# One kernel, four small edits: the column sum of the values on GpSimd and in slot 6, the gelu table asked for early, the second inverse roots moved, and fill products in the first image

## The chip, the cores and the metric

The kernel runs on one core of one Trainium2 chip. The metric is the device time of one execution, in microseconds. The median of three runs before the change is 2034.94 us (2033.91 to 2036.55). The profiled execution took 2021.73 us, with a span of 2020.0 us from the first to the last instruction.

The engines are called by the profile's names: PE (TensorE, the matmuls), PEld (its weight loads), DVE (VectorE), ACT (ScalarE), POOL (GpSimd), SP (SyncE, which here only issues DMAs).

## What is computed

Sixteen images and sixteen texts of 128 tokens go through a small model. Cut to what matters:

```
h  = concat(edge_filter(image) [256 rows x 256], (U*s @ Vt)[text ids] [128 rows x 256])   # 384 rows
h  = h + attention(layernorm(h))       # 16 heads of 16, window of 128 keys back
h  = h + gated_block(layernorm(h))     # gelu(x @ w_block) in the 288 best rows, x in the others
h  = h + state_space(layernorm(h))     # circulant recurrence over the rows
h  = h + shared_ffn(x) + two_of_eight_experts(x),  x = layernorm(h)

attn = softmax(scores) + 1e-9          # so ctx = softmax @ v + 1e-9 * (sum of v over all 384 rows)
ffn(x) = gelu(x @ w1.T + b1) @ w2.T + b2
layernorm(x) = (x - mean) / sqrt(var + 1e-5)
```

The 1e-9 matters for this change: every row of the attention's output gets 1e-9 times the sum of all value rows, and the kernel computes that sum.

## The kernel before, in words

**Two halves.** The first (to about 1400 us of the span) goes through the images, one after another; the second does the experts in chunks of 256 rows. The change touches the first half only.

**Slots.** One image's attention is cut into 24 units (3 tiles of 128 query rows, 8 pairs of heads). `sequence(b, ...)`, which exists once for each engine, walks through 33 slots (`SLOTS`, s from 0 to 32), and in each it writes out, in a fixed order, what the engine does there: in slot s the scores of unit s on PE, its row maximum on DVE, its exp on ACT, then the transposes of the probabilities of unit s-2 on PE and their copy out of PSUM on ACT. Every fourth slot, 6, 10, 14 and so on, has the products of four units' probabilities with the values. Slots 0 to 7 work on 128 keys, slots 8 to 23 on 256 keys. Between these lie, in fixed slots, the pieces of three other images: the tail ("chain") of image b-1, that is gate, block, state space and router; the second half of the shared feed-forward of image b-2 (`DOWNS`: six pieces in slots 2, 3, 4, 5, 7 and 8); and the head of image b+1, that is edges, text rows, projections. Engines meet through semaphores only. Each engine works strictly in its own written order, so an instruction that waits holds up everything behind it.

The trip of the steady images, b = 2 to 13 or 14, is a loop. Images 0 and 1 and the last ones are written out apart. Image 0 has no chain and no shared feed-forward around it; there DVE also works out, in slots 1 to 10, the powers of the rotation for the state space (`eigenvalues`, `powers`), many small steps each waiting for the last.

**What the change touches.**

- `values_sum`: PE multiplies a constant matrix (`ones9`, all 1e-9) with the three tiles of values in `vaug`, adding up in PSUM bank 5. Tile 0 is done in slot 1 (`TURN0`), tiles 1 and 2 in slot 2 (`BLOCK`). DVE copies the result to `sumv` in slot 2. It is first read in slot 13.
- Slots 1 and 2 of PE: turned rows of the chain (`turn_chain`), the scores 1, the ranks of image b-2 (`slot_ranks`), then the row of gate scores (line 1840), the block's product (line 1790), and the first piece of the shared feed-forward (line 1813). That last piece waits until ACT has read the block's product through gelu (`g`, line 876), since both lie in the same banks.
- ACT holds one table of functions at a time. Exp and gelu are in different ones. In every image the exp's table is loaded behind `g`, and the gelu's ahead of the first `hidden_layer` (line 885, slot 30), behind the copy `cxT` (line 857). On PE `up(b, f)` (line 1800) makes the hidden layer's product f in one of two banks in turn; `up(b, 2)` waits until ACT has read product 0.
- `deviations` on DVE: eleven small steps on 3 numbers a row (lines 1087 to 1093), each waiting for the one before. For the chain's second layernorm they stand behind the row maximum of slot 8, while the statistics (lines 1075 to 1079) stand in slot 7 ahead of the maximum of slot 7. Their result is used in slot 11 (`chain_scale`), whose rows PE turns in slot 12 (line 1785).
- `keep_warm(n)`: PE multiplies the identity with itself n times into a bank that nobody reads.
- POOL's `sequence`: the six scattered stores of `dispatch`, then the direct term and one part of the states, inverse roots for the head, the residuals, and last in the image the gather of text rows and `hbo` (line 641).

## Time and profile before

| what | us |
|---|---|
| median of three runs | 2034.94 |
| lowest, highest | 2033.91, 2036.55 |
| profiled execution: its time | 2021.73 |
| profiled execution: span | 2020.0 |
| PE busy | 1887.5 (93% of the span) |
| DVE busy | 1395.3 (69%) |
| ACT busy | 1068.6 (53%) |
| POOL busy | 741.4 (37%) |
| one steady image (from the text product at 704.28 to the next at 785.00) | 80.72 |

A row of a timeline has the start, the time, the engine, the line and operation with output and input, how many in a row, and in square brackets how long the engine had been idle before it and who ended that. PE's own instructions overlap: the next may start before the modelled end of the last, so the distance from start to start is what one takes of the engine. A row of stretches has from and to, the length, the busy time of PE, PEld, DVE, ACT and POOL with their counts, PE's granted clock (1.00 is 2.4 GHz, 0.50 is 1.2 GHz), the DMA's share and GB/s.

### The profile page before, as it was taken

What the parts mean: (1) busy time and instruction counts of PE and PEld (TensorE: products, weight loads), DVE (VectorE), ACT (ScalarE), POOL (GpSimd) and SP (SyncE); (2) the same over time, 40 slices, a digit from 0 to 9 for tenths busy, and PEclk for the clock granted to TensorE, in tenths of its full rate; (3) what the DMA queues carried; (4) which work ended last, traced back from release to release, by engine and by line L of the source; (5) the groups of instructions that cost most, each with busy time, mean ns of one, the idle gap of its engine ahead of it and who ended that gap; (6) DMA issues with size and microseconds to landing.
All of it is one profiled execution on the core that took longest, in us unless ns stands there. A gap on an engine that the chain in (4) does not pass through costs nothing.

```text
span 2020.0 us, 46113 instructions
## 1 busy us (share of the span) xinstructions
PE 1887.5 (93%) x14343; PEld 1639.6 (81%) x14344; DVE 1395.3 (69%) x3963; ACT 1068.6 (53%) x2511; POOL 741.4 (37%) x1074
## 2 busy tenths in 40 slices
PE   5769999999999999999999999888999999999997
PEld 5557787777777877777778777677999999999997
DVE  6768778777787787787877876764765565655653
ACT  1545556556555565565555655622655555645643
POOL 2003334233333342333333322314554454555554
PEclk9889999999999999999999999988999999999999
DMA  4321131220211312202213122012432332423322
GB/s 141 86 49 51 30 73 37 51 70 25 64 52 29 72 38 50 70 25 64 52 28 72 39 49 55 9 58 69 140 92 42 47 90 43 90 44 88 48 46 39
DMA packets 81148, 117.04 MB, mean 58 GB/s; under 512 B 20964, under 2 KB 61508, under 8 KB 78724
## 3 DMA queue, kind: packets, MB, share of 16 engines
q1 hardware_dynamic: 54372, 84.16, 15.6%
q0 software_dynamic: 23360, 27.91, 8.4%
q10 hardware_dynamic: 3312, 3.94, 0.7%
q14 instruction: 82, 0.67, 0.1%
q8 instruction: 22, 0.36, 0.1%
HBM read 51.58 MB, written 26.71 MB: 39 GB/s over the span
## 4 chain that ended last, share of the span: by engine, by line
PE 68%; DVE 11%; issue 10%; ACT 4%; POOL 3%; SPq 1%; ACTq 1%; DVEq 0%; POOLq 0%; DMA 0%
PE ps L1996 15%; PE ps L1800 6%; PE ps L2007 5%; PE ps L1813 5%; PE ps L2008 5%; PE ps L2009 5%; PE ps L1728 3%; PE ps L1632 3%; PE ps L1717 2%; PE ps L1718 2%; PE ps L1790 2%; PE ps L1851 2%; DVE mx L1215 2%; PE ps L1785 2%; PE ps L1666 2%
## 5 line engine op out<-in xcount | busy, mean ns | idle before, releaser
L849 ACT ACTIVATE prob<-ps,mx 128x256 f32<-128x256 f32 (+1 forms) x768 | 295.7, 445 | 125.6 <-DVE mx L1215 112.7
L969 ACT ACTIVATE hid_hi<-ps,b 128x256 fp32r<-128x256 f32 x408 | 205.8, 504 | 276.3 <-PE ps L1996 276.3
L1215 DVE TENSOR_REDUCE mx<-ps 128x2 f32<-128x512 f32 (+1 forms) x384 | 228.7, 597 | 152.2 <-PE ps L1718 124.9
L841 ACT ACTIVATE pT<-ps 128x512 f32<-128x512 f32 (+1 forms) x384 | 203.5, 535 | 191.2 <-PE ps L1728 190.3
L1562 DVE TENSOR_TENSOR hid_lo<-hid_full,hid_hi 128x256 fp32r<-128x256 f32 x408 | 171.2, 426 | 143.6 <-ACT hid_full L972 143.0
L762 POOL DMA_INDIRECT result<-yb,idx_o x102 | 179.9, 1763 | 164.0 <-DVE yb L1579 147.5
L2007 PE MATMUL ps<-w_hi,hid_hi 128*128 128x256 f32 x816 | 230.0, 282 | 0.0
L2008 PE MATMUL ps<-w_lo,hid_hi 128*128 128x256 f32 x816 | 225.5, 276 | 0.0
L2009 PE MATMUL ps<-w_hi,hid_lo 128*128 128x256 f32 x816 | 225.3, 276 | 0.0
L1728 PE MATMUL ps<-ident,prob 128*128 128x128 f32 x1280 | 208.7, 278 | 5.5 <-ACT prob L849 5.4
L972 ACT ACTIVATE hid_full<-ps,b 128x256 f32<-128x256 f32 x408 | 206.2, 505 | 0.0
L1728 PEld LDWEIGHTS ps<-ident,prob 128*128 128x128 f32 x1280 | 160.8, 142 | 50.7 <-ACT prob L849 12.8
L1718 PE MATMUL ps<-ks,qs 96*128 96x512 f32 (+1 forms) x384 | 199.7, 520 | 0.0
L1813 PE MATMUL ps<-sw,hid 128*128 128x256 f32 x768 | 182.9, 383 | 2.3 <-ACT g L876 1.0
L706 POOL DMA_INDIRECT slot_rows<-pay,row_i x96 | 109.6, 1142 | 191.5 <-DVE tok L1408 167.0
L1717 PE MATMUL ps<-mask_bf,ident_bf 128*128 128x512 bf16 (+1 forms) x384 | 135.7, 353 | 41.4 <-ACT prob L849 27.7
L1996 PE MATMUL ps<-xg_hi,w_hi 128*128 128x256 f32 x816 | 165.1, 284 | 2.5 <-issue 1.2
L1813 PEld LDWEIGHTS ps<-sw,hid 128*128 128x128 f32 x768 | 140.8, 191 | 29.5 <-issue 6.2
L1996 PE MATMUL ps<-xg_hi,w_lo 128*128 128x256 f32 x816 | 164.4, 283 | 0.0
L1996 PE MATMUL ps<-xg_lo,w_hi 128*128 128x256 f32 x816 | 164.4, 283 | 0.0
L2008 PEld LDWEIGHTS ps<-w_lo,hid_hi 128*128 128x128 f32 x816 | 153.4, 188 | 0.0
L2007 PEld LDWEIGHTS ps<-w_hi,hid_hi 128*128 128x128 f32 x816 | 153.3, 188 | 0.0
(321 smaller groups left out, 4333.7 us busy)
## 6 DMA issues: line engine op xcount, KB each, us to landing
w_raw<-in_w SPq DMA_DIRECT2D x16, 1024.0 KB, 5.9
xin<-in_x SPq DMA_DIRECT2D x32, 384.0 KB, 3.8
ks<-k_hi SPq DMA_DIRECT2D x256, 48.0 KB, 2.1
qs<-q_hi SPq DMA_DIRECT2D x120, 96.0 KB, 2.2
ks<-k_lo SPq DMA_DIRECT2D x128, 48.0 KB, 2.1
xn_rows<-xc SPq DMA_DIRECT2D x16, 384.0 KB, 2.5
result<-h SPq DMA_DIRECT2D x16, 384.0 KB, 2.6
qs<-q_lo SPq DMA_DIRECT2D x60, 96.0 KB, 2.1
```

The costliest lines, as they stand in the source:

```text
L841: act.activation(pT[:, u % TB, :, k0:2, :], ps[:, 2 + u % 2, :].rearrange("p (h k q) -> p h k q", h=2, k=2)[:, :, k0:2, :], ACT.Copy).then ...
L849: ins = act.activation(prob[:, s % PB, hh, w], ps[:, s % 2, hh * 2 * P + w.start:(hh + 1) * 2 * P], ACT.Exp, bias=mx[:, s % 2, hh:hh + 1])
L969: act.activation(hid_hi[:, f], ps[:, f % 4, 0:CHUNK], ACT.Gelu_apprx_tanh, bias=b1[half][:, f:f + 1])
L972: act.activation(hid_full[:, f % 4], ps[:, f % 4, 0:CHUNK], ACT.Gelu_apprx_tanh, bias=b1[half][:, f:f + 1]).then_inc(ehid_ready.sem, 1)
L1215: dve.tensor_reduce(mx[:, s % 2], sc, AX_X, ALU.max, negate=True).then_inc(max_done.sem, 1)
L1718: pe.matmul(dst, qs[:, r, m, i * P:(i + 1) * P], ks[:, r, :, m, keys], start=False, stop=True).then_inc(scores_done.sem, 1)
L1728: ins = pe.transpose(ps[:, 2 + u % 2, (2 * hh + k) * P:(2 * hh + k + 1) * P], prob[:, u % PB, hh, k * P:(k + 1) * P], ident[:])
L1813: ins = pe.matmul(tile_out(i), hid[:, f, i * P:(i + 1) * P], sw2[:, f], start=(f == 0), stop=(f == FB - 1))
L1996: ins = pe.matmul(ps[:, f % 4, 0:CHUNK], w[half][:, k, cols], x[:, k], start=(n == 0), stop=(n == len(terms) - 1))
L2007: pe.matmul(out, hid_hi[:, f, rows], w2_hi[half][:, f], start=(f == 0), stop=False)
L2008: pe.matmul(out, hid_hi[:, f, rows], w2_lo[half][:, f], start=False, stop=False)
L2009: ins = pe.matmul(out, hid_lo[:, f, rows], w2_hi[half][:, f], start=False, stop=(f == FB - 1))
```

## The change

1. **Values.** POOL adds the three tiles of values of image b into `vsum`, a view of `ctx_t`, at the start of its image, in two steps; PE multiplies `ones9` with `vsum` once, in slot 6 (`SUMV`); DVE copies the result in slot 7. The three products in slots 1 and 2, and the copy in slot 2, are gone.
2. **Gelu's table.** ACT runs a gelu on one column into a tile that nobody reads, in slot 28, in the images that have both an attention and a chain (1 to 15).
3. **Second roots.** The eleven steps for the chain's second layernorm stand right behind the statistics in slot 7.
4. **Fill products.** In image 0 only, PE runs 20 products of the identity ahead of the scores of slot 2, and 8 behind the scores of each of the slots 3 to 14, into bank 6.

```diff
+SUMV = 6
+        vsum = ctx_t[:].rearrange("p g q -> p (g q)")[:, 0:D]
...
+            def add_values(b):
+                heads = vsum.rearrange("p (h d) -> p h d", h=NH)
+                pool.wait_ge(v_ready.sem, v_ready.at(b, 1))
+                pool.tensor_tensor(heads, vaug[:, 0, :, 0:DK], vaug[:, 1, :, 0:DK], ALU.add).then_inc(vsum_step.sem, 1)
+                pool.wait_ge(vsum_step.sem, vsum_step.at(b, 1))
+                pool.tensor_tensor(heads, heads, vaug[:, 2, :, 0:DK], ALU.add).then_inc(vsum_ready.sem, 1)
...
             def sequence(b, att, late, chain, head, ahead):
+                if att:
+                    add_values(b)
...
+                    if att and chain and s == TURN2 + 1:
+                        act.activation(gelu_spare[:], sb1[:, 0:1], ACT.Gelu_apprx_tanh)
...
                 if s == RANK + NT + 3:
-                    chain_rows(b, 1)
+                    chain_rows(b, 1, True)
...
-                    if att and s == 2:
+                    if att and s == SUMV + 1:
                         values_sum(b)
                     if att:
                         unit(b, s)
-                    if chained and s == RANK + NT + 4:
-                        dve.wait_ge(stats_ready.sem, stats_ready.at(b - 1, 2))
-                        deviations(lnc, rstd_ready, chain_step, b - 1)
...
-            def values_sum(b, first, last):
-                pe.wait_ge(v_ready.sem, v_ready.at(b, 1))
+            def values_sum(b):
+                pe.wait_ge(vsum_ready.sem, vsum_ready.at(b, 1))
                 pe.wait_ge(h1_ready.sem, h1_ready.at(b, 0))
-                for i in range(first, last):
-                    ins = pe.matmul(ps[:, 5, D:2 * D].rearrange("p (h d) -> p h d", h=NH), ones9[:], vaug[:, i, :, 0:DK],
-                                    start=(i == 0), stop=(i == NT - 1))
-                if last == NT:
-                    ins.then_inc(sumv_done.sem, 1)
+                pe.matmul(ps[:, 5, D:2 * D], ones9[:], vsum, start=True, stop=True).then_inc(sumv_done.sem, 1)
...
-                    if att and s == BLOCK:
-                        values_sum(b, 1, NT)
...
+                    if first and not chained and s == BLOCK:
+                        keep_warm(20, 6)
                     if att:
                         unit_scores(b, s)
-                    if att and s == TURN0:
-                        values_sum(b, 0, 1)
+                    if first and not chained and BLOCK < s < CONV:
+                        keep_warm(8, 6)
+                    if att and s == SUMV:
+                        values_sum(b)
```

PE in the loop of the steady images, slots 1 and 2, before; `ones` is the constant matrix, the REGISTER_ALU and ISA rows are waits:

```order
L1718 MATMUL ps<-ks,qs 128x2x128
L1698 REGISTER_ALU
L1699 ISA
L1701 MATMUL ps<-vaug,ones 128x256
L1826 MATMUL ps<-hot,ltri 128x24
...
L1840 MATMUL ps<-xcT,wr_bc 128x384 x2
L1790 MATMUL ps<-wb,xcT 128x256 x4
L1844 ISA
L1790 MATMUL ps<-wb,xcT 128x256 x2
L1701 MATMUL ps<-vaug,ones 128x256 x2
...
L1813 MATMUL ps<-sw,hid 128x256 x4
```

The same engine now, from the scores of slot 1 to the first piece of the shared feed-forward, and then slot 6:

```order
L1728 MATMUL ps<-ks,qs 128x2x128
L1833 REGISTER_ALU
L1836 MATMUL ps<-hot,ltri 128x24
...
L1850 MATMUL ps<-xcT,wr_bc 128x384 x2
L1800 MATMUL ps<-wb,xcT 128x256 x4
L1854 ISA
L1800 MATMUL ps<-wb,xcT 128x256 x2
...
L1823 MATMUL ps<-sw,hid 128x256 x4
...
L1713 ISA
L1714 MATMUL ps<-ctx_t,ones 128x256
L1738 MATMUL ps<-ident,prob 128x128 x2
L1758 MATMUL ps<-pT,vaug 32x128 x8
```

The three products left slots 1 and 2, and one came in slot 6, between its scores and the transposes.

DVE in the same loop, slots 7 to 9, before; `mx` is a row maximum, `lnc` holds statistics and roots:

```order
L1079 BN_AGGR lnc<-lnc 128x2 x3
L1214 REGISTER_ALU
L1215 TENSOR_REDUCE mx<-ps 128x2
...
L1215 TENSOR_REDUCE mx<-ps 128x2
L1444 ISA
L1087 TENSOR_SCALAR lnc<-lnc 128x3
...
L1093 SCALAR_TENSOR_TENSOR lnc<-lnc 128x3
L1214 REGISTER_ALU
L1215 TENSOR_REDUCE mx<-ps 128x2
```

DVE there now:

```order
L1096 BN_AGGR lnc<-lnc 128x2 x3
L1255 ISA
L1104 TENSOR_SCALAR lnc<-lnc 128x3
...
L1110 SCALAR_TENSOR_TENSOR lnc<-lnc 128x3
L1225 COPY sumv<-ps 128x256
L1231 REGISTER_ALU
L1232 TENSOR_REDUCE mx<-ps 128x2
L1231 REGISTER_ALU
L1232 TENSOR_REDUCE mx<-ps 128x2
```

The eleven steps and the copy of the sum now stand ahead of the maximum of slot 7, where the steps stood behind that of slot 8.

ACT at the end of a steady image, before, and behind it now; `hid` is the first hidden layer's gelu:

```order
L869 ACTIVATE xcT_hi<-ps 128x768
L855 REGISTER_ALU
L857 ACTIVATE cxT<-ps 128x256
L884 REGISTER_ALU
L885 ACT_TABLE_LOAD
L885 ACTIVATE hid<-ps,sb 128x384
```

```order
L884 ACTIVATE xcT_hi<-ps 128x768
L947 ACT_TABLE_LOAD
L947 ACTIVATE gelu_spare<-sb 128x1
L870 REGISTER_ALU
L872 ACTIVATE cxT<-ps 128x256
L899 REGISTER_ALU
L900 ACTIVATE hid<-ps,sb 128x384
```

The table load moved from between `cxT` and `hid` to ahead of `cxT`; the number of table loads in an image is the same.

## Rows read from the trace of the kernel before

**Rows 1.** The page: busy time of the engines.
```profile
PE 1887.5 (93%) x14343; PEld 1639.6 (81%) x14344; DVE 1395.3 (69%) x3963; ACT 1068.6 (53%) x2511; POOL 741.4 (37%) x1074
```
**Rows 2.** Timeline of PE, a steady image, slots 1 and 2.
```profile
770.84 0.60 PE L1701 MATMUL ps<-vaug,ones 128*128 128x256 f32 x2
...
771.75 1.56 PE L1840 MATMUL ps<-xcT,wr_bc 128*128 128x384 f32 x4 [0.23 <-ACT xcT L869]
...
775.74 1.03 PE L1701 MATMUL ps<-vaug,ones 128*128 128x256 f32 x4
776.80 1.99 PE L1813 MATMUL ps<-sw,hid 128*128 128x256 f32 x8
```
**Rows 3.** Timeline of ACT, same place.
```profile
775.94 0.81 ACT L876 ACTIVATE g<-ps 128x768 f32<-128x768 f32 x1 [2.10 <-PE ps L1790]
```
**Rows 4.** Timeline of PE, same image, slots 9, 10 and 12.
```profile
792.94 0.38 PE L1717 MATMUL ps<-mask_bf,ident_bf 128*128 128x512 bf16 x1
...
794.31 0.39 PE L1717 MATMUL ps<-mask_bf,ident_bf 128*128 128x512 bf16 x1 [0.54 <-ACT prob L849]
...
797.06 0.87 PE L1785 MATMUL ps<-ident,xc 128*128 128x128 f32 x6
```
**Rows 5.** Timeline of DVE, same image, slots 7 to 9.
```profile
790.01 0.39 DVE L1215 TENSOR_REDUCE mx<-ps 128x2 f32<-128x256 f32 x1
791.19 0.69 DVE L1215 TENSOR_REDUCE mx<-ps 128x2 f32<-128x512 f32 x1 [0.79 <-PE ps L1718]
791.80 0.16 DVE L1087 TENSOR_SCALAR lnc<-lnc 128x3 f32<-128x3 f32 x1
...
793.88 0.69 DVE L1215 TENSOR_REDUCE mx<-ps 128x2 f32<-128x512 f32 x1
```
**Rows 6.** Timeline of ACT, same image, exp of slots 7 and 8.
```profile
791.10 0.62 ACT L849 ACTIVATE prob<-ps,mx 128x128 f32<-128x128 f32 x2
...
793.42 0.84 ACT L849 ACTIVATE prob<-ps,mx 128x256 f32<-128x256 f32 x2
```
**Rows 7.** Timeline of DVE: the copy of the sum, and the maximum behind it.
```profile
777.12 0.42 DVE L1208 COPY sumv<-ps 128x256 f32<-128x256 f32 x1
779.19 0.42 DVE L1215 TENSOR_REDUCE mx<-ps 128x2 f32<-128x256 f32 x1 [1.65 <-PE ps L1718]
```
**Rows 8.** Timeline of ACT, end of a steady image.
```profile
760.66 0.39 ACT L857 ACTIVATE cxT<-ps 128x256 f32<-128x256 f32 x1 [5.72 <-PE ps L1763]
761.06 1.28 ACT L885 ACT_TABLE_LOAD   x1
762.36 1.05 ACT L885 ACTIVATE hid<-ps,sb 128x384 f32<-128x384 f32 x2
```
**Rows 9.** Timeline of PE: line 1735 at the image's end, and in slot 17.
```profile
761.51 1.02 PE L1735 MATMUL ps<-wo,cxT 128*128 128x256 f32 x4
762.99 0.62 PE L1800 MATMUL ps<-xcT_hi,sw_hi 128*128 128x384 f32 x2 [0.45 <-ACT hid L885]
```
```profile
728.58 1.03 PE L1735 MATMUL ps<-wo,cxT 128*128 128x256 f32 x4
729.44 0.38 PE L1717 MATMUL ps<-mask_bf,ident_bf 128*128 128x512 bf16 x1
```
**Rows 10.** Timeline of PE: an earlier fill of 24 products, and slot 2 of image 0.
```profile
30.13 5.62 PE L1941 MATMUL ps<-ident 128*128 128x128 f32 x48
...
56.59 0.28 PE L1717 MATMUL ps<-mask_bf,ident_bf 128*128 128x256 bf16 x1 [2.79 <-DMA ks<-k_lo]
```
**Rows 11.** Stretches of image 0, its slots 3 to 14 (columns as told above).
```profile
57.00:75.50 18.50, 13.52 (x77) 8.13 (x75) 17.08 (x92) 8.77 (x27) 0.00 (x0) 0.63 0.38 123
75.50:83.00 7.50, 4.95 (x59) 3.69 (x58) 5.86 (x12) 7.50 (x16) 0.00 (x0) 1.00 0.01 4
```
**Rows 12.** Timeline of POOL around the loop's turn, and a part of the states.
```profile
768.67 2.26 POOL L641 TENSOR_TENSOR hbo<-h,bo_row 128x256 f32<-128x256 f32 x3 [11.62 <-DVE xc L1100]
782.29 1.36 POOL L706 DMA_INDIRECT slot_rows<-pay,row_i  x1 [11.36 <-DVE tok L1408]
```

More of the change, by code:

```diff
@@ L124, in build @@
         spare = sb("spare", [P, 1])
+        gelu_spare = sb("gelu_spare", [P, 1])
         c15 = sb("c15", [P, NT])
@@ L326, in build @@
         v_ready = signal("v_ready", 1)
+        vsum_step = signal("tiles_of_values_added", 1)
+        vsum_ready = signal("vsum_ready", 1)
         sumv_done = signal("sumv_done", 1)
@@ L1935, in sequence, with keep_warm @@
                     up(b - 1, f)
-            def keep_warm(count):
+            def keep_warm(count, bank=5):
                 for n in range(count):
-                    pe.matmul(ps[:, 5, 0:P], ident[:], ident[:], start=True, stop=True)
+                    pe.matmul(ps[:, bank, 0:P], ident[:], ident[:], start=True, stop=True)
             for sig in signals:
```

## The prediction

> **What bounds the kernel now.** I read the page's busy times first. PE is busy 93% of the span [rows 1], so what counts is where PE really waits, and whom for. Then I read one steady image (80.72 us, fourteen of them) engine by engine, at the places that the edits touch. Three things are to be seen.
>
> In slots 1 and 2 PE waits for ACT, twice, and the removed products lie just ahead of both waits. Line 1840 starts when ACT's copy of the turned rows is done, 0.23 us after PE ran out of work [rows 2]. Line 1813 starts at 776.80; the gelu `g` that it must wait for runs from 775.94 to 776.75 [rows 2, 3].
>
> In slots 7 to 10 PE and DVE take turns. DVE has nothing to spare from slot 3 to the maximum of slot 7; PE waits 0.54 us for an exp ahead of slot 10, and turns the rows of slot 12 as soon as DVE has them [rows 4, 5].
>
> At the image's end ACT is idle 5.72 us, copies `cxT`, loads the gelu's table and only then runs the first gelu; PE has finished line 1735 by then and waits [rows 8, 9].
>
> The first image is another matter: there DVE is the bound. In the 18.50 us from 57.0 it is busy 17.08, while PE is busy 13.52 at a granted clock of 0.63, a mixture of its two levels [rows 11].
>
> **The products of the values.** Removed in slot 1: one product, 0.43 us from start to start; in slot 2: two, 0.86 us, since four passes of line 1735 with the same width take 729.44 - 728.58 = 0.86 [rows 2, 9]. That is 1.29 us of PE in each image. But `g` can't start earlier: it started with the end of line 1790, before the removed products were done. Without them PE comes to line 1813 at 775.9 instead of 776.6 and waits until 776.8 as now. The same holds in slot 1: line 1840 keeps its start at 771.75, with a wait of 0.66 instead of 0.23. Gain: nothing. The cover is the waits themselves.
>
> Added in slot 6: one product, 0.43 us of PE (two passes, as in slot 1). No wait stands around it that hides it all. The products of the four units behind it wait at present some 0.15 us for a copy by ACT, and that swallows part. I take 0.25 us, between 0 and 0.43.
>
> The additions stand first in POOL's image. POOL ends `hbo` at 770.93 and then idles 11.36 us until the stores [rows 12]. Two additions of the size of one of the three in line 641 (2.26 / 3 = 0.75 us each) end near 773 to 776 and are wanted in slot 6, at 787. Price 0. What is queued behind them on POOL, `dispatch`, starts at 782.29 anyway.
>
> The Trainium skill ("GPSIMD Engine Reference", Key points) says that POOL shares its SBUF interfaces with VectorE, and that they get in each other's way when DVE has two SBUF inputs. No row of mine has this pair of operations. By that rule DVE's counting in slots 1 and 2 would run up to 1.5 us longer, and the idle 1.65 us ahead of slot 2's maximum [rows 7] would take it in; the sum stays.
>
> **The copy and the roots on DVE.** The copy of the sum (0.42 us, 0.34 until the next starts) leaves slot 2, where DVE idles 1.65 us right behind it [rows 7]: gain 0. It comes to slot 7. The eleven root steps take 793.88 - 791.80 = 2.08 us [rows 5] and now stand ahead of slot 7's maximum too. So that maximum goes from 790.01 to 790.15 + 2.08 + 0.34 = 792.6, and ends at 793.0. Queued behind it: the maxima of slots 8 and 9 and the sum of line 1380. Who waits: exp of slot 7 on ACT (0.62 us, now at 791.10) [rows 6] then ends at 793.7 instead of 791.7, and the scores of slot 9 on PE, which start at 792.94 [rows 4], wait for it: they start 0.8 us later. Of this the 0.54 us of idle ahead of slot 10 gives something back. Exp of slot 8, now 793.42, starts behind exp 7 and the copy of the transposes, at 793.9; so slot 10 starts at 794.78 instead of 794.31. From there on the eleven steps are out of DVE's way, but the maximum of slot 9 is late by as much, and the rows of slot 12 are turned at 797.5 instead of 797.06. Sum for the slot-6 product, the copy and the roots together: **+0.47 us** an image. With the roots left where they were the product and the copy alone would cost 0.25. The bounds: 0 (the loop finds its slack elsewhere) and 0.8. Fifteen images: +7.0 us, between 0 and 12. PE is without any wait of this size from slot 12 to slot 18, so I see nothing that gives it back.
>
> **The gelu's table.** The load (1.28 us) moves from between `cxT` and the first gelu into ACT's 5.72 us of idle [rows 8]; it is covered there, 4 us over. The first gelu then runs at 761.06 and ends by 761.6. PE's next product waits for nothing more and starts when line 1735 lets it: 761.51 + 0.86 = 762.38 instead of 762.99. Gain **0.61 us** an image [rows 9]. Next late would be the rows that DVE gives for the next image, ready 0.6 us before PE takes them at present, so the gain just fits. Bounds: the listed idle, 0.45, and 0.8. Fifteen images (1 to 15): -9.2 us, between -6.7 and -12.
>
> **The fill in image 0.** 24 such products took 5.62 us at the full clock, 0.234 us each [rows 10]. Eight: 1.87 us, in twelve slots 22.5 us; twenty: 4.7 us. The twenty have the 2.79 us that PE idles for a DMA ahead of slot 2's scores [rows 10] and the 1.29 us of the removed products, 4.1 us in all; 0.6 us is lost. Slots 3 to 14 last at present from 57.0 to 83.0, 26.0 us. PE's own work in them: 4.95 us of the last 7.5 us at the full clock; 13.52 us at 0.63 is about 8.5 at full; together 13.5 us by busy time, 12.0 by start-to-start distances, which is the tighter count since ends are modelled [rows 11]. With the fill 12.0 + 22.5 = 34.5 us. So PE takes DVE's place as the bound, and slot 15 begins 8.5 + 0.6 = **9.1 us** later. Bounds: 8 and 11. What the fill may bring is the clock: PE would no longer fall to 1.2 GHz. But behind that fall DVE was busy 17.08 of 18.5 us, so PE's speed was not what image 0 waited for; from 75.5 on the clock is at 2.4 GHz anyway.
>
> The Trainium skill ("TensorE: Matmul & The Clock Gate", Why this matters for your kernels) advises to leave no long idle gaps on PE, so as to keep the clock up. By that rule the fill is a gain: at most the 13.52 - 8.5 = 5 us that PE's work takes longer. The trace agrees on the clock and not on the time, by DVE's busy share.
>
> **The sum** against the profiled execution: 2021.73 + 9.1 + 7.0 - 9.2 = 2028.6, that is +6.9 us. The median of the runs is 2034.94, 13.2 us more than the profiled execution; the same difference on it gives 2041.8. I say **2042**.
>
> **Rivals.**
> - *The fill costs nothing.* PE's fill would hide behind DVE's steps. For it: DVE's busy share. Against: 34.5 us of PE do not go into 26.0. Then +7.0 - 9.2 = -2.2: 2033; with the full clock gain of 5 us 2028. Chance 0.12 for both.
> - *Faster: the removed products were on the path.* Then each image loses 1.29 us more, 15 x 1.29 = 19.4: 2042 - 19 = 2023. It decides from 0.73 us an image on. For it: PE's 93%. Against: the two waits right behind the products. Chance 0.06.
> - *The clock stays at 1.2 GHz under the fill.* Then eight products take 3.7 us, and image 0 costs some 20 us more: 2062. Against: the earlier fills ran at full clock. 0.04.
> - *POOL's additions hold DVE up* where it has no cover, or they come late for slot 6. At 0.8 us an image 12 us more: 2054. 0.04.
> - *The change doesn't do what it says:* the table load might have stayed where it was; then the gain of 9.2 is gone: 2051. The instruction order shows it moved. 0.01.
>
> **How the numbers follow.** My forecast has 0.73, with an own range of 2035 to 2050: lows and highs of the three terms don't fall together. The range for 8 in 10 takes in the first rival's 2033: 2033 to 2050. A measurement of this kernel can tell about 0.2%, 4.1 us. Slower by more (over 2039.0): 0.60 of my 0.73, and the two slow rivals and the last: 0.69. Within: 0.12 of mine and 0.07 of the first rival: 0.19. Faster by more: 0.01 of mine, 0.05 of the first rival, 0.06 of the second: 0.12.
>
> **What would show it.** In the profile after: slot 15 of image 0 starts near 92 with PE busy without a break and a granted clock of 1.00 before it. In a steady image line 1823 (the old 1813) still waits for `g`, now with 0.8 us or more of listed idle; the gelu's table load lies in the idle ahead of `cxT`, and the third product of the hidden layer follows line 1735 without a wait; the scores of slot 9 wait for an exp. A steady image lasts 80.6 us. I am wrong if image 0 is not longer, or if a steady image differs from 80.72 by more than 0.5.

## The result and the profile after

The changed kernel is **slower**: 2050.3 us (median of six runs, 2046.5 to 2056.8) against 2034.2 us for the kernel before (six runs beside them, 2028.9 to 2036.5). The medians differ by 16.1 us. The ratio is 1.0090, with a 95% interval of 1.0076 to 1.0104; on 2034 us that is 18.3 us (15.5 to 21.2). Forecast were 2042 us, 7 more than before, and a range of 2033 to 2050: the direction was right, the size was not.

The profiled execution took 2049.4 us (span 2047.6), 27.7 more than that of before. By its trace 1.05 us of this lie ahead of the first image's text product, 16.8 between that product and the last turn of rows of the last image, and 9.8 behind it, in the experts' part, none of whose instructions the change touches.

On the page PE's busy time has grown by 17 us from [rows 1]: 116 fill products of 0.223 us (26 us) came, 16 x 0.86 us of the products of the values (14 us) went, and the experts' part has 9.6 us more (634.2 against 624.6). That would be 21.6; the 4.3 that are missing are for the most part PE's own products of image 0, which are shorter at the full clock: image 0 from 46.5 us on has PE busy 19.5 us longer with 26 us of fill in it, and a granted clock of 1.00 for 0.81.

```profile
PE 1904.8 (93%) x14511; PEld 1666.4 (81%) x14512; DVE 1397.1 (68%) x3963; ACT 1069.7 (52%) x2526; POOL 750.9 (37%) x1106
```

**Slots 1 and 2** (timeline of PE, then ACT, then POOL, one steady image that starts slot 0 at 949.63). They answer to [rows 2, 3].

```profile
951.74 1.56 PE L1850 MATMUL ps<-xcT,wr_bc 128*128 128x384 f32 x4 [0.65 <-ACT xcT L884]
953.13 2.75 PE L1800 MATMUL ps<-wb,xcT 128*128 128x256 f32 x12
956.79 0.48 PE L1823 MATMUL ps<-sw,hid 128*128 128x256 f32 x1 [0.90 <-ACT g L891]
```
```profile
955.92 0.81 ACT L891 ACTIVATE g<-ps 128x768 f32<-128x768 f32 x1 [2.10 <-PE ps L1800]
```
```profile
951.58 0.73 POOL L720 TENSOR_TENSOR ctx_t<-vaug 128x256 f32<-128x256 f32 x1
952.38 0.73 POOL L722 TENSOR_TENSOR ctx_t<-ctx_t,vaug 128x256 f32<-128x256 f32 x1
```

The time of the removed products has become idle time: line 1850 waits 0.65 us where its twin waited 0.23, and line 1823 waits 0.90 for `g`. POOL's additions take 0.73 us each and lie where it idled. DVE's row maximum beside the second of them took 0.42 us, as before [rows 7]:

```profile
952.68 0.42 DVE L1232 TENSOR_REDUCE mx<-ps 128x2 f32<-128x256 f32 x1 [3.02 <-issue]
```

DVE's next step (953.86) starts after the additions, so no row here has POOL adding beside a step of DVE with two inputs in SBUF, the case that the prediction priced.

**Slots 6 to 12**, same image, DVE, ACT and PE. They answer to [rows 4 to 6].

```profile
972.22 0.17 DVE L1110 SCALAR_TENSOR_TENSOR lnc<-lnc 128x3 f32<-128x3 f32 x1
972.30 0.42 DVE L1225 COPY sumv<-ps 128x256 f32<-128x256 f32 x1
972.64 1.01 DVE L1232 TENSOR_REDUCE mx<-ps 128x2 f32<-128x256 f32 x2
```
```profile
973.09 0.63 ACT L864 ACTIVATE prob<-ps,mx 128x128 f32<-128x128 f32 x2 [1.42 <-DVE mx L1232]
```
```profile
967.38 0.60 PE L1714 MATMUL ps<-ctx_t,ones 128*128 128x256 f32 x2
...
973.77 0.39 PE L1727 MATMUL ps<-mask_bf,ident_bf 128*128 128x512 bf16 x1
...
974.88 0.39 PE L1727 MATMUL ps<-mask_bf,ident_bf 128*128 128x512 bf16 x1 [0.27 <-ACT prob L864]
...
977.61 0.87 PE L1795 MATMUL ps<-ident,xc 128*128 128x128 f32 x6
```

From slot 0's turn the scores of slot 9 start after 24.14 us (973.77 - 949.63), before after 23.31; the rows of slot 12 are turned after 27.98, before after 27.43.

**The image's end**, ACT then PE, to be held against [rows 8, 9].

```profile
935.64 1.28 ACT L947 ACT_TABLE_LOAD   x1
936.94 0.20 ACT L947 ACTIVATE gelu_spare<-sb 128x1 f32<-128x1 f32 x1
941.35 0.38 ACT L872 ACTIVATE cxT<-ps 128x256 f32<-128x256 f32 x1 [4.21 <-PE ps L1773]
941.63 0.58 ACT L900 ACTIVATE hid<-ps,sb 128x384 f32<-128x384 f32 x1
```
```profile
942.20 1.02 PE L1745 MATMUL ps<-wo,cxT 128*128 128x256 f32 x4
942.87 0.70 PE L1810 MATMUL ps<-xcT_hi,sw_hi 128*128 128x384 f32 x2
```

The load is covered with 4 us to spare, and the third product of the hidden layer follows line 1745 without a wait.

**Image 0** (stretches, columns as ahead of the prediction; then PE's first edge product of slot 15). It answers to [rows 11].

```profile
60.00:80.00 20.00, 20.00 (x179) 18.81 (x178) 16.57 (x91) 7.39 (x24) 0.00 (x0) 1.00 0.35 112
80.00:100.00 20.00, 20.00 (x179) 17.51 (x178) 10.82 (x18) 12.34 (x25) 0.00 (x0) 1.00 0.01 2
```
```profile
93.91 0.40 PE L1646 MATMUL ps<-gray_hi,band_hi 128*128 128x512 f32 x1
```

PE has no gap, at full clock, and DVE has: the bound has changed sides. Slot 15 began at 83.40 before.

**Two things that nobody had asked for.** In slot 6 of twelve of the loop's thirteen passes ACT idles 1.9 to 2.7 us ahead of a copy whose input has long been there (the transposes at 967.82 took 0.38 us), and the profile finds no release on this core; in the last pass it doesn't idle there:

```profile
970.15 0.39 ACT L856 ACTIVATE pT<-ps 128x256 f32<-128x256 f32 x1 [1.89 <-remote]
...
1210.56 0.38 ACT L856 ACTIVATE pT<-ps 128x256 f32<-128x256 f32 x1
```

Slots 0 to 12 take 28.0 to 29.05 us in those passes, 28.53 in the mean, and jump about; before, the same twelve took 27.42 to 27.44 and the last one 27.12. And the experts' products are slower, at the same granted clock of 1.00 and without an idle moment (page, count, busy, mean ns). This row is of the changed kernel, the one below it of a profile of the kernel before:

```profile
L2019 PE MATMUL ps<-w_hi,hid_hi 128*128 128x256 f32 x816 | 233.5, 286 | 0.0
```
```profile
L2007 PE MATMUL ps<-w_hi,hid_hi 128*128 128x256 f32 x816 | 230.0, 282 | 0.0
```

### The profile page after: what moved, and what is told of

It is laid out like the page before. It is cut to its first block, busy times and chain, and to the rows that moved or that the text cites. A ratio compares the mean times of both kernels' runs of the same rounds, so it can differ in the third digit from the quotient of the medians.

```text
span 2047.6 us, 46471 instructions
## 1 busy us (share of the span) xinstructions
PE 1904.8 (93%) x14511; PEld 1666.4 (81%) x14512; DVE 1397.1 (68%) x3963; ACT 1069.7 (52%) x2526; POOL 750.9 (37%) x1106
## 3 DMA queue, kind: packets, MB, share of 16 engines
q1 hardware_dynamic: 54372, 84.16, 15.5%
## 4 chain that ended last, share of the span: by engine, by line
PE 71%; DVE 11%; issue 6%; ACT 5%; POOL 3%; SPq 1%; another core or an unknown queue 1%; ACTq 1%; DVEq 0%; POOLq 0%; DMA 0%
PE ps L2008 14%; PE ps L1810 7%; PE ps L2020 5%; PE ps L2021 5%; PE ps L2019 5%; PE ps L1738 4%; PE ps L1823 3%; PE ps L1646 3%; PE ps L1727 2%; ACT prob L864 2%; PE ps L1728 2%; PE ps L1680 2%; PE ps L1800 2%; PE ps L1861 2%; PE ps L1795 2%
## 5 line engine op out<-in xcount | busy, mean ns | idle before, releaser
L2021 PE MATMUL ps<-w_hi,hid_lo 128*128 128x256 f32 x816 | 229.4, 281 | 0.0
L711 POOL DMA_INDIRECT slot_rows<-pay,row_i x96 | 97.7, 1018 | 159.5 <-DVE tok L1425 135.0
```

What stands on the lines that cost most here:

```text
L2021: ins = pe.matmul(out, hid_lo[:, f, rows], w2_hi[half][:, f], start=False, stop=(f == FB - 1))
```

## The experiments

All runs in one table. A, B, C, D are the four parts: values, gelu's table, roots, fill. "Image 0" is from the first text product to slot 15's first edge product; "image 1" and "steady" are slots 0 to 12; "end" is slot 27 to slot 0; "experts" is from the last turn of rows to the end of the span. Times in us; the ratio is to the kernel before, timed beside each (2015 to 2025 us beside e1 to e16, 2029 to 2032 beside e17 and e18). "Steady" is the mean of the loop's passes but the last. In "image 0" the sixteen kernels that don't have the whole fill go from 58.9 to 64.2 us, so a single value there tells little below 5 us.

| kernel | image 0 | image 1 | steady | end | experts | median | ratio |
|---|---|---|---|---|---|---|---|
| before | 60.2 | 27.0 | 27.43 | 17.81 | 644.4 | | |
| changed | 69.7 | 30.1 | 28.53 | 17.08 | 654.3 | 2050.3 | 1.0090 |
| e1 A B C | 62.5 | 29.2 | 27.99 | 17.09 | 655.0 | 2033.3 | 1.0051 |
| e2 B | 61.3 | 27.3 | 27.42 | 17.09 | 653.7 | 2021.8 | 1.0001 |
| e3 A C | 64.2 | 30.3 | 27.99 | 17.80 | 644.9 | 2041.9 | 1.0100 |
| e4 D | 70.7 | 26.3 | 27.43 | 17.78 | 654.0 | 2042.5 | 1.0101 |
| e5 changed again | 70.4 | 29.5 | 28.00 | 17.09 | 653.8 | 2042.6 | 1.0084 |
| e6 A | 60.9 | 26.6 | 27.79 | 17.79 | 653.8 | 2035.7 | 1.0054 |
| e7 C | 58.9 | 28.9 | 27.75 | 17.80 | 654.2 | 2034.7 | 1.0057 |
| e8 B again | 60.9 | 26.3 | 27.43 | 17.09 | 654.9 | 2020.8 | 0.9986 |
| e9 two products less | 60.5 | 26.4 | 27.42 | 17.79 | 644.6 | 2022.2 | 0.9998 |
| e10 A, copy later | 60.2 | 26.7 | 28.12 | 17.80 | 653.9 | 2043.3 | 1.0110 |
| e11 B, half a fill | 61.9 | 26.5 | 27.43 | 17.08 | 644.7 | 2022.2 | 1.0001 |
| e12 before | 62.5 | 26.5 | 27.43 | 17.81 | 644.3 | 2023.0 | 1.0001 |
| e13 the tile alone | 59.0 | 26.3 | 27.42 | 17.78 | 654.0 | 2033.4 | 1.0056 |
| e14 B, tile last | 60.1 | 27.3 | 27.42 | 17.05 | 644.1 | 2011.4 | 0.9940 |
| e15 changed, tile last | 68.2 | 29.8 | 27.99 | 17.05 | 643.1 | 2029.7 | 1.0041 |
| e16 extra product | 59.6 | 26.6 | 27.66 | 17.80 | 644.7 | 2025.2 | 1.0020 |
| e17 tile of 8 bytes | 60.6 | 26.3 | 28.15 | 17.77 | 654.1 | 2042.4 | 1.0060 |
| e18 B, gap of 56 bytes | 60.1 | 26.5 | 28.13 | 17.07 | 649.5 | 2024.4 | 0.9966 |

### Which part costs what

e1 leaves the two `keep_warm` calls of image 0 out of the changed kernel; e2 is the kernel before with the gelu of slot 28; e3 has A and C; e4 has the two `keep_warm` calls alone.

> The changed kernel without its fill in image 0 (parts A, B and C stay). The two traces put slot 15 of image 0 at 83.40 before and 93.91 after, of which 1.05 us is a later start. Theory 1 (the fill costs its length where DVE had been the bound): slot 15 is back within 1 us of 83.4 and the time falls by 9.5 us against the changed kernel, some 2041 against 2050. Theory 2 (the fill also sets image 1 back, where the turn of slot 12 came 3.1 us later after slot 0 than before): 12 us or more come back. Rival (the fill gives the clock back later and costs less than its length): under 7 us. In both theories the loop's images keep 28.0 to 29.0 us from slot 0 to slot 12 (before 27.43), and ACT's idle of 1.9 to 2.7 us ahead of the copy of pT in slot 6 stays.

> The kernel before with part B alone: one gelu on one column of ACT in slot 28. Slots 27 to 0 go from 17.81 to 17.1 us in each of 15 images, -10.5 us. Theory 1 (the new idle of ACT in slot 6, which ends with no release that the profile shows, comes from ACT's own instructions, of which the loop now holds one more): a stall of 2 to 3 us stands in 12 of the 13 passes of the loop in this kernel too, at the same copy or near it, and slots 0 to 12 take over 27.43. Theory 2 (it comes from A or C): no such stall, slots 0 to 12 stay at 27.43 and the time is 10 us below that before, 2024.

> Parts A and C alone, without the early gelu and without the fill; ACT's instructions are those of the kernel before. Theory 1 (the stall belongs to ACT's longer loop): no stall in slot 6, slots 0 to 12 take 27.4 to 27.7 us as in the last pass of the loop of the changed kernel (27.37), time 1 to 5 us above before. Theory 2 (the stall belongs to A or C): slots 0 to 12 at 28.0 to 29.0, 12 stalls, time 14 to 18 us above before.

> The kernel before with the fill alone. With the three products of the values still in slots 1 and 2, 0.9 to 1.3 us more stand ahead of slot 3 than in the changed kernel. Theory 1: slot 15 of image 0 starts 9.5 to 11 us later than 83.4, and the time is 10 to 11 us above before. Theory 2 (image 1 is set back too): 13 us or more. Rival (clock regained): under 7 us.

In these four kernels the columns of the images add up. e1's slot 15 is 7.9 us earlier than that of the same kernel with the fill (e5). The fill: slot 15 comes after 70.7 us in e4 and after 60.8 in the mean of the fifteen runs without a fill (58.9 to 64.2). The four with the whole fill have 68.2 to 70.7, in the mean 69.75: +9.0. A and C: +0.56 in a steady image. B: -0.71 at the image's end. Theory 1 of e2 and of e3 fell: the idle time in slot 6 is neither in e2 nor in e1, which has the same ACT instructions as the changed kernel; and theory 2 of e3 fell as well, since its passes took 27.99 without a stall, not 28.0 to 29.0 with one. e1 met none of its theories: slot 15 began at 86.95 and not near 83.4, the loop's passes have no idle time in slot 6, and its time is 17 us below that of the changed kernel, but beside other times of the kernel before; by the ratios (1.0090, and 1.0084 in e5, against 1.0051) it is 7 to 8 us. In e4 image 0 is 10.4 us longer than before, as its theory 1 has it, and image 1 isn't set back (26.3). But the times don't follow the images. From the first text product to the last turn of rows e2 is 8.5 us faster than before and its time is that of before; e4 is 12 us slower and its time is 21 us up. What eats the gain is the column of the experts: 653.7 against 644.4.

### The changed kernel again, its parts A and C apart, part B again

e6 is A alone, e7 C alone.

> The changed kernel itself once more. The same kernel without the fill showed no idle time of ACT without a release ahead of the copy of pT in slot 6, and 27.97 to 28.03 us from slot 0 to slot 12; ACT's and DVE's instructions are the same in both. Theory 1 (the stall belongs to one loading of the program, not to a part of the change): this run shows slots 0 to 12 at 28.0 in every pass of the loop and no such idle time. Theory 2 (it comes with the fill together with A to C): 28.0 to 29.0 again, and 12 idle times of 1.9 to 2.7 us. For the experts' part, from the last turn of rows of the last image to the end: before 644.5 us, changed kernel 654.2; theory 1 lets it be either, theory 2 says 654.

> Part A alone (additions on GpSimd, one product in slot 6, the copy of the sum in slot 7). A and C together made slots 0 to 12 of a steady image 0.56 us longer (27.99 against 27.43). Forecast by the retiming of the prediction: A alone 0.25, so 27.7. Rival 1: A's product and copy take all of it, 27.99. Rival 2: A costs nothing as long as the roots are not in slot 7, 27.43 or below. Image 1, slots 0 to 12: 27.0 to 27.5 if its 2 to 3 us come from the roots, 29 or more if they come from A.

> Part C alone (the eleven root steps directly behind the statistics in slot 7). Forecast by the retiming: some 0.2 to 0.3 us more from slot 0 to slot 12, 27.7. Rival 1: the roots take all of the 0.56, 27.99. Rival 2: none, 27.43. Image 1, slots 0 to 12 (before 27.02): 29 or more if the roots make it longer there.

> Part B alone, a second time. In the first run its images were 10 us faster than those of before by the trace, but the experts' part took 653.7 us against 644.5, with the same instructions at the same granted clock, and the time was that of before. Theory 1 (each loading of a program takes one of two paces in the experts' part, whatever the kernel): this run may end near 2011 to 2013 with 644.5, or near 2021 with 654. Theory 2 (B itself slows the experts' part down): 653 to 654 again and a ratio of 1.000.

e5 has no such idle time of ACT and 27.97 to 28.03 us in every pass but the last: theory 1. The stall was not a part of the change, and no run found what it was.

A alone costs 0.36, C alone 0.32 (forecast: 0.25 and 0.2 to 0.3), both 0.56. Image 1 tells them apart: 26.6 with A, 28.9 with C. There the roots stand ahead of the maximum that PE is waiting for, and PE has no shared feed-forward of an image b-2 to do meanwhile (e7, DVE and PE, then the same wait of PE in e8):

```profile
146.38 1.01 DVE L1217 TENSOR_REDUCE mx<-ps 128x2 f32<-128x256 f32 x2
```
```profile
147.51 0.39 PE L1716 MATMUL ps<-mask_bf,ident_bf 128*128 128x512 bf16 x1 [2.63 <-ACT prob L851]
```
```profile
148.27 0.39 PE L1721 MATMUL ps<-mask_bf,ident_bf 128*128 128x512 bf16 x1 [0.80 <-ACT prob L851]
```

2.63 - 0.80 = 1.8 us, close to the 2.08 of the eleven steps. Held against slot 0's turn, the scores of slot 9 of image 1 start after 21.8 to 22.0 us in every kernel without A and C, after 22.2 with A, 24.1 with C and 24.5 with both (25.1 in e15): up to there the parts cost 2.6 us. From these scores to slot 12's turn it is PE's clock that tells: 4.4 us at a granted 1.00 (e8) and 5.4 at 0.54 (e14), where neither has A or C (stretches, columns as ahead of the prediction); with both parts 4.7 at 0.64 (e1) to 5.8 at 0.50 (e3). So of the 3.2 us that image 1 is longer in the mean, some 0.6 lie in this stretch, where all five kernels with both parts had a clock of 0.50 to 0.66.

```profile
148.27:152.66 4.39, 3.39 (x32) 2.36 (x33) 4.05 (x16) 3.07 (x9) 0.13 (x1) 1.00 0.00 0
```
```profile
146.29:151.66 5.37, 5.37 (x32) 3.69 (x33) 4.24 (x18) 3.92 (x10) 0.88 (x2) 0.54 0.01 3
```

e8's ten runs went from 2010.6 to 2026.9 us, wider than those of before beside it (2018.5 to 2024.2), so its pace in the experts' part may have differed from run to run; only the profiled one can be looked into, and it had 654.9.

### The removed products, the copy, half a fill

e9 drops the products of tiles 1 and 2 of the values:

```diff
-                for i in range(first, last):
-                    ins = pe.matmul(ps[:, 5, D:2 * D].rearrange("p (h d) -> p h d", h=NH), ones9[:], vaug[:, i, :, 0:DK],
-                                    start=(i == 0), stop=(i == NT - 1))
+                pe.matmul(ps[:, 5, D:2 * D].rearrange("p (h d) -> p h d", h=NH), ones9[:], vaug[:, 0, :, 0:DK],
+                          start=True, stop=True).then_inc(sumv_done.sem, 1)
...
-                    if att and s == BLOCK:
-                        values_sum(b, 1, NT)
```

e10 is e6 with DVE's copy behind the maximum of slot 8; e11 is e2 with `keep_warm(8, 6)` ahead of slot 2's scores and `keep_warm(4, 6)` behind the others'.

```diff
-                    if att and s == SUMV + 1:
-                        values_sum(b)
                     if att:
                         unit(b, s)
+                    if att and s == SUMV + 2:
+                        values_sum(b)
```

> The kernel before without the two products of the values in slot 2 (0.86 us of PE); the third one, in slot 1, stays. The sum then holds one tile of values of three, so this kernel leaves out two thirds of that sum. Theory (the products stood ahead of a wait and were never on the path): slots 0 to 12 stay at 27.43 us and line 1813, the first of the products behind g, waits for g for 0.8 us or more. Rival (they were on the path in part): slots 0 to 12 at 26.6 to 27.2.

> Part A alone, with DVE's copy of the sum behind the maximum of slot 8 instead of ahead of the maximum of slot 7. A with the copy in slot 7 took 27.79 us from slot 0 to slot 12 against 27.43. Theory 1 (the copy takes its 0.34 us in front of the chain maximum 7, exp 7, scores 9): 27.43 to 27.55. Theory 2 (the product in slot 6 takes its 0.43 us of PE): 27.79 stays. Both in part: 27.6 to 27.7.

> Part B with a fill of half the size: 8 products ahead of the scores of slot 2 of image 0 and 4 behind those of slots 3 to 14, 56 products, 12.5 us at 0.223. PE's own 12 us and the fill then are 24.5 us in slots 3 to 14, which took 26.0 with DVE as the bound. From the first product of the text to slot 15, image 0 took 58.9 to 64.2 us in the runs without a fill and 69.7 to 70.7 in those with the whole one. Theory 1 (the fill costs only what does not fit beside DVE): 59 to 63 us. Rival 1 (each product of the fill costs its length): 66 or more. Rival 2 (with the clock at 2.4 GHz image 0 is shorter than without a fill): 58 or less, and image 1, slots 0 to 12, at 26.3 as in the run with the fill alone.

> The kernel before itself, with a profile on this chip. Its 35 timed runs on two chips were 2018 to 2025 us, which its images (1375 us) and an experts' part of 644.5 us give; the trial kernels mostly took 654 us for the same instructions. Theory 1 (each run takes one of two paces by itself): the profile may show 644 or 654, and the runs of this kernel, loaded as a trial kernel, may be near 2021 or near 2031. Theory 2 (the pace belongs to the kernel): 644 and 2018 to 2025 in all runs.

**e9**: 27.42 us against 27.43. The 0.86 us were worth nothing. The page shows where they went, into 0.9 us of waiting in each of the fifteen images that have a block ahead (the row of before has 1.0 us for `g` in all):

```profile
L1810 PE MATMUL ps<-sw,hid 128*128 128x256 f32 x768 | 182.9, 383 | 14.3 <-ACT g L876 13.7
```

**e10** missed every theory of mine: 28.12, that is 0.33 more than with the copy in slot 7. DVE in its slots 8 and 9:

```profile
308.18 0.69 DVE L1230 TENSOR_REDUCE mx<-ps 128x2 f32<-128x512 f32 x1 [1.03 <-PE ps L1729]
308.79 0.41 DVE L1223 COPY sumv<-ps 128x256 f32<-128x256 f32 x1
309.12 0.16 DVE L1102 TENSOR_SCALAR lnc<-lnc 128x3 f32<-128x3 f32 x1
...
311.20 0.69 DVE L1230 TENSOR_REDUCE mx<-ps 128x2 f32<-128x512 f32 x1
```

Between the maxima of slots 8 and 9 lie the copy and the roots, 3.02 us from start to start, where before it were 2.69 [rows 5]: the copy's 0.33 are in full on the path. I had looked at DVE's idle time ahead of maximum 8 and not at what stands behind it.

**e11**: 61.9 us, inside the spread of the runs without a fill (58.9 to 64.2). Half a fill costs nothing that this spread would show, theory 1. It gains nothing either, though PE was at full clock: DVE remained the bound, with 18.50 us of 20 busy.

```profile
60.00:80.00 20.00, 17.66 (x157) 14.86 (x157) 18.50 (x94) 10.94 (x30) 0.00 (x0) 1.00 0.35 112
```

**e12**: before, profiled once more, has 644.3 us, and its ten runs are 2019 to 2024, theory 2.

### The experts' part: a tile of 4 bytes

By now three profiles of kernels without the new tile (before, e12, e9) had 644.3 to 644.6 us, and nine of eleven with it 653.7 to 655.0 (e3 and e11 were the exceptions). e13 is the kernel before and one line, whose tile nobody uses. e14 is part B, and e15 the changed kernel, with the tile allocated as the last of the image phase, where it moves no other. e16 asks the other open question, with one more product in slot 6.

```diff
         spare = sb("spare", [P, 1])
+        gelu_spare = sb("gelu_spare", [P, 1])
```
```diff
-        gelu_spare = sb("gelu_spare", [P, 1])
...
         h4 = room("h4", [P, NT, D])
+        gelu_spare = room("gelu_spare", [P, 1])
```
```diff
+            def extra_product(b):
+                pe.wait_ge(sumv_ready.sem, sumv_ready.at(b, 1))
+                pe.matmul(ps[:, 5, D:2 * D].rearrange("p (h d) -> p h d", h=NH), ones9[:], vaug[:, 0, :, 0:DK],
+                          start=True, stop=True)
...
+                    if att and s == 6:
+                        extra_product(b)
```

> The kernel before with the changed kernel's extra tile of 4 bytes a partition, allocated at the same place and used by nobody; every instruction is that of the kernel before, only the addresses of the tiles behind it move by 4 bytes. Theory 1 (addresses set the pace of the experts' products): an experts' part of 654 us, or timed runs in two groups, near 2021 and near 2031. Theory 2 (the pace comes from the instructions that the parts add or reorder): 644.5 and 2018 to 2025 in all runs.

> Part B alone, with its tile of one column allocated behind the last tile of the image phase, so that no other tile's address moves. Theory 1 (addresses): an experts' part of 644.5 us, all timed runs at 2010 to 2014, a ratio of 0.995, faster than before. Theory 2 (instructions): timed runs in two groups again, near 2012 and near 2022, ratio near 1.000.

> The changed kernel with the tile of part B allocated behind the last tile of the image phase. Theory 1 (addresses): an experts' part of 644.5 us, timed runs at 2031 to 2035, 10 to 12 us above before, which is what the change costs by its images. Theory 2 (instructions): 654 us and runs near 2042.

> The kernel before with one more product of the width of the one that part A puts in slot 6 (0.43 us), at the same place ahead of slot 6's transposes; nobody reads its result. DVE's copy stays in slot 2. Slots 0 to 12 take 27.43 us without it and 27.79 with part A. Theory 1 (PE's product is what costs): 27.7 to 27.8. Theory 2 (the copy ahead of the maximum of slot 7 costs): 27.43 to 27.5. Both in part: in between.

Theory 1 held in e13, e14 and e15. With the same instructions and every later tile moved by 4 bytes, e13 takes 654.0 us for the experts and 2033.4 in all, 11.6 us more than before (1.0056, interval 1.0039 to 1.0072). With the tile last, e14 has 644.1 us and 2011.4: **the fastest kernel here**, 0.994 of before (0.9923 to 0.9956). e13's row, and e14's:

```profile
L2008 PE MATMUL ps<-w_hi,hid_hi 128*128 128x256 f32 x816 | 233.5, 286 | 0.0
```
```profile
L2011 PE MATMUL ps<-w_hi,hid_hi 128*128 128x256 f32 x816 | 230.0, 282 | 0.0
```

The whole change without the shift (e15) costs 8.3 us (0.0041 x 2021.87), a little less than expected.

The address doesn't decide alone, though. e3 and e11 have the tile in the old place and kept the fast pace (644.9 and 644.7 us; e11's row is that of e14):

```profile
L2015 PE MATMUL ps<-w_hi,hid_hi 128*128 128x256 f32 x816 | 230.1, 282 | 0.0
```

And in kernels with the tile there the runs of one and the same program fall into two groups: e11's ten are 2012.2 and 2014.7, the second of them the profiled one with 644.7, and eight from 2020.8 to 2027.1; e1's are 2022.7 and 2023.7, and eight from 2032.2 to 2038.2. The medians of the groups lie 9 to 10 us apart, about the 9.6 us between the two paces. So the shift makes the slow pace the usual one (eleven of thirteen profiles with 4 or 8 bytes, none of six without a shift); what chooses between the paces from run to run was not found.

**e16**: 27.66, +0.23 for the product alone. A is 0.36, so 0.13 are left for the rest of A, most likely the copy ahead of maximum 7; that is a difference, and no run has the copy alone. Both in part.

### What about the shift

> The kernel before with an unused tile of 8 bytes a partition at the place where a tile of 4 bytes made the experts' part 654.0 us and the time 2033. Theory 1 (what counts is that the experts' operands start at a multiple of 8 bytes, where before they do by my count of the tiles ahead of them): 644 to 645 us, timed runs at 2018 to 2025. Theory 2 (any shift from the old addresses does it): 654 us, runs near 2032.

> Part B with its tile last, as in the run that took 2011 us, and with an unused gap of 56 bytes a partition, which by my count brings the experts' tiles from 8 bytes past a multiple of 64 to a multiple of 64. Theory 1 (8 bytes are all that counts): experts' part 644 to 645, 2008 to 2014 as without the gap. Theory 2 (a wider alignment counts too): an experts' part below 640 us. Rival (any shift slows it down): 654 and 2021.

e17 is e13 with `[P, 2]`, e18 is e14 with a tile `[P, 14]` behind `spare`. Theory 1 of e17 fell: 8 bytes do the same as 4, 654.1. e18 has 649.5 and a mean of 284 ns, a third value, which fits neither theory. So of the four offsets tried (0, 4, 8 and 56 bytes) the one that before happens to have is the only one that was slow in no profile, and what makes it so stays open.

The loop was odd too, in both kernels: 28.15 and 28.14 in the mean of the passes but the last (27.13 in both). In e17 the maximum of slot 7, whose scores PE had begun at 631.40, starts late on DVE, which was free at 633.1:

```profile
632.88 0.21 DVE L1080 BATCH_NORM_AGGREGATE lnc<-lnc 128x2 f32<-128x6 f32 x2
634.59 1.02 DVE L1216 TENSOR_REDUCE mx<-ps 128x2 f32<-128x256 f32 x2 [1.50 <-PE ps L1719]
```

It resembles ACT's stall in the first profile: one engine, one place, every pass but the last. But it isn't bound to the loop: image 15, which is written out apart, has it as well (DVE idle for 1.53 us where e13 has 0.80, slots 0 to 12 in 27.40 us for 26.63). The kernel before ran at 2029 to 2032 us beside e17 and e18, 9 us more than beside the others, and 13 times 0.7 us would be 9.1. That it had the same stall was not seen, as it wasn't profiled there.

## Why the prediction was right or wrong

The step that failed is the sum itself: it adds up what the images gain and lose and has no term for the experts' part, which it puts at nothing without giving a reason. That part took 9.6 us more. A second, smaller miss is the image 1 among its "fifteen images": 3.2 us for the 0.47 forecast.

| term | forecast | measured |
|---|---|---|
| fill | +9.1 | +9.0 |
| A and C, images 2 to 15 | 14 x 0.47 = +6.6 | 12 x 0.56 + 0.25 + 0.15 = +7.1 |
| A and C, image 1 | +0.4 | +3.2 (29.8, five runs with both, against 26.6, fourteen without the roots) |
| gelu's table | -9.2 | 15 x -0.71 = -10.6 (fourteen seen; the end of image 15 takes 15.3 to 17.6 us, whatever the kernel) |
| sum | +6.9 | +8.7 |
| the tile's place | none | +9.6 |

- **The removed products: gain nothing.** Right, by the waits in the trace and by e9.
- **A and C, +0.47.** Right in size and place: scores 9 were forecast 0.8 us late and came 0.83 late, and an exp is what they wait for (that of slot 7 ends at 973.72). By itself A was under-sized (0.36 for 0.25): the product took 0.23 by e16, and the other 0.13 were not counted.
- **Image 1.** The step that said "fifteen images" took image 1 for a steady one. It is written out apart and has less work on PE, so what the steps and the copy add to DVE is in full on the path: 2.6 us by the scores of slot 9. The rest of the +3.2 comes behind them, at a granted clock of 0.50 to 0.66, which the prediction didn't look at in image 1.
- **The table.** Right in mechanism, 0.71 for 0.61: line 1745 and the products behind it moved together, and no next wait stood behind them.
- **The fill.** The mechanism is right: PE without a gap, as the bound in DVE's place. That +9.0 stands beside +9.1 is in part luck. From the scores of slot 3 to slot 15 the changed kernel takes 34.4 us (59.52 to 93.91), forecast were 34.5; but the 96 products took 0.223 us each (21.4, for 22.5), so PE's own work was 13.0 and not 12.0, and the two misses cancel. And the mean without a fill (60.8) is one of values that lie 5 us apart. The Trainium skill ("TensorE: Matmul & The Clock Gate", Why this matters for your kernels) would keep PE's gaps short for the clock's sake; the rows agree on the clock (1.00 in e11 with half a fill, for the 0.63 of [rows 11]) and show no gain in time, since DVE had the work.
- **The sum.** 2021.73 + 6.9 was the forecast for the profiled execution; the change by itself costs 8.3 (e15) to 8.7. This agreement is no closer than the traces allow: from the first text product to the last turn of rows e15 takes 6.3 us more than before and e5 11.2, image 0 and the last images' ends being what varies. The term that is missing is the experts' part: the declaration of a 4-byte tile, which I had read as free, moved all operands of the second half (e13: 654.0 for 644.4 with no other edit), and +8.7 + 9.6 = 18.3 is 0.9% of 2034. That this meets the ratio of 1.0090 to the digit is luck: the changed kernel's profiled execution had ACT's stall on top, and the kernel before took 12.5 us more than its own profiled execution, neither of which is in the sum. Without the stall (e5) the ratio is 1.0084, that is 17.0 us, with an interval of 11.3 to 22.7.
- **The steady image**, forecast 80.6: 28.00 + 35.53 + 17.09 = 80.62 in e5. In the first profile it was 81.13 in the mean (28.53 + 35.53 + 17.08), 12 of the passes having ACT's stall. That stall (12 x 0.53 = 6.4 us in the passes; from the first text product to the last turn 1369.1 against 1363.6 in e5) is in that profile, but not in the change.

**Open** remain the stall's cause; why the kernel before took 2034 us beside the changed kernel, 12.5 us more than its own profiled execution and 11 to 13 more than the medians of its runs beside e1 to e16 (it may have had the slow pace or a stall in those runs; the profiled execution has neither); and why two kernels with the tile kept the fast pace.

## What to carry to other kernels

Count a new tile as an edit of its own: put it last, or look at the stages behind it in the trace before you believe a gain or a loss. Cost a step at its every place: the written-out first and last passes of a loop have other neighbours and another bound than the steady one. Fill products cost here what didn't fit, with PE's own work, beside the engine that was the bound (+9.0 us for 116, nothing to be seen for 56), and bought nothing, since another engine was the bound.

## What the runs showed of the hardware

- A matmul of 128x128 by 256 columns took 276 to 282 ns in the experts' part without a shift of its operands in SBUF, and 281 to 286 in eleven of thirteen profiles with one of 4 or 8 bytes a partition (276 to 282 in e3 and e11; 279 to 284 with 56 bytes, e18). The products of the experts' first layer, between them, kept 283 to 284 in all.
- Each pass of the loop but the last takes some 0.3 us more in slots 0 to 12 (27.43 against 27.12 before). At the start of most passes the profile shows two or three packets of the instruction queue and an idle time of DVE of 3.0 to 3.2 us, for which in some it names no engine; in the last pass one packet, and DVE waits 0.91 us for PE. These two things are not shown to belong together: the loop's first pass (image 2) has no such packet and 1.08 us of idle time, and took 27.42 as well, and in the stretches shown the scores of slot 3 start 11.97 us after slot 0's turn in either pass; the difference comes behind them. The stretches are 1091.5 to 1095.7 and 1172.3 to 1176.5 of the kernel before, DMA queues and timeline of DVE:

```profile
q14 instruction: 3, 0.02, 2.2%
```
```profile
1095.11 0.42 DVE L1215 TENSOR_REDUCE mx<-ps 128x2 f32<-128x256 f32 x1 [3.16 <-issue]
```
```profile
q14 instruction: 1, 0.01, 0.5%
```
```profile
1173.60 0.42 DVE L1215 TENSOR_REDUCE mx<-ps 128x2 f32<-128x256 f32 x1 [0.91 <-PE ps L1718]
```

  Whether the stalls of ACT and of DVE in single runs are of this kind was not shown; that of DVE in e17 stands in image 15 too, outside the loop.
- The Trainium skill ("ScalarE: Activation LUTs", What ACT_TABLE_LOAD costs) counts a drain of some 1.4 us to a table switch. The trace here shows the load's 1.28 us, 0.02 us behind the end of ACT's last copy (934.78 + 0.84 = 935.62), and the gelu 1.30 behind its start (935.64 to 936.94); no drain is seen on either side:

```profile
934.78 0.84 ACT L884 ACTIVATE xcT_hi<-ps 128x768 fp32r<-128x768 f32 x1
```
